# One transpose buffer instead of two, and all attention masks loaded at once as bf16

## What is computed

```python
def _L0_attn_ref(x, Wq, Wk, Wv, Wo, bo, Wconv):
    kc = conv_general_dilated(x.transpose(0,2,1), Wconv, window_strides=(3,), padding='VALID', ...)
    k_tmp = concatenate([x[:, :1, :], kc], axis=1)            # 1366 keys
    mask = (k_idx[None, :] * 3.0 >= q_idx[:, None] + 0.001)
    q, k, v = x @ Wq.T, k_tmp @ Wk.T, k_tmp @ Wv.T            # 16 heads of 64
    scores = einsum('bhqd,bhkd->bhqk', q, k) * HD ** (-0.5) + mask * -1000000000.0
    o = einsum('bhqk,bhkd->bhqd', softmax(scores), v)
    return o.reshape(b, t, d) @ Wo.T + bo
def _L0_ffn_ref(x, ...):                                      # w1, w2: 4096x1024; h1, h2: 4096x4096; w3: 1024x4096
    h = silu(tlin(x, w1_w, w1_s)) * tlin(x, w2_w, w2_s)
    h = gelu(tlin(h, h1_w, h1_s)); h = gelu(tlin(h, h2_w, h2_s))
    return tlin(h, w3_w, w3_s)
x = x + layernorm(_L0_attn_ref(layernorm(x), ...))
x = x + layernorm(_L0_ffn_ref(layernorm(x), ...))
```

## Time and profile before

| | us |
|---|---|
| median of the 2 runs | 6467.4 (6462.9 to 6471.9) |
| profiled execution | 6481.0 |
| its slowest core, core 3 (first to last instruction) | 6479.5 |
| its other cores | 6429.4 to 6447.9 |
| TensorE busy / VectorE / ScalarE, core 3 | 3206.5 / 705.8 / 599.9 |
| busy time of the 16 DMA engines, SP's queue / POOL's queue | 40.7% / 17.4% of the span |

### The profile page before, as it was taken

The page is one execution under the profiler, slowest core; times in us unless marked ns, Lnnn a source line. Parts: engine busy times, 40 slices in busy tenths (PEclk is TensorE's granted clock), DMA queues, the critical chain, the costliest instruction groups (busy, mean ns, idle before and its releaser), DMA issues.

```text
span 6479.5 us, 38888 instructions; the slowest of 8 cores (6429.4 to 6479.5 us)
## 1 busy us (share of the span) xinstructions
PE 3206.5 (49%) x15168; PEld 1447.2 (22%) x15168; DVE 705.8 (11%) x1430; ACT 599.9 (9%) x881; POOL 89.7 (1%) x176
## 2 busy tenths in 40 slices
PE   0000044651001020234425999489985999669994
PEld 0000011220000010112202444134432444224441
DVE  0014400101001010111044000110001100020001
ACT  0000000010001010223211100011000100011000
POOL 0000000000000000010000000000000000000000
PEclk9999987875555555555567999789997999889997
DMA  9963345339999999960244555256543555345552
GB/s 128 121 130 99 98 78 84 52 52 208 110 146 186 141 166 196 211 151 4 62 107 117 149 142 145 75 140 156 141 121 96 143 146 153 96 117 145 143 143 78
DMA packets 1378643, 805.86 MB, mean 124 GB/s; under 512 B 607248, under 2 KB 1338528, under 8 KB 1364128
## 3 DMA queue, kind: packets, MB, share of 16 engines
q1 hardware_dynamic: 1360352, 610.44, 40.7%
q0 software_dynamic: 18112, 192.95, 17.4%
HBM read 618.73 MB, written 236.98 MB: 132 GB/s over the span
## 4 chain that ended last, share of the span: by engine, by line
PE 46%; DMA 24%; another core or an unknown queue 11%; SPq 8%; DVE 4%; issue 4%; ACT 2%; DVEq 0%; POOL 0%; ACTq 0%; POOLq 0%
PE ps_f L1140 28%; PE ps_f L1078 6%; DMA p2b<-n_h 5%; DMA wbuf<-t_w 4%; PE ps_f L1198 4%; DMA t_h<-p2b 4%; PE ps_cv L462 3%; SPq L697 3%; DMA cv_nat<-wconv 2%; ACT pt_sb L802 2%; DMA lx<-x_full 2%; DVE ln_st L311 2%; SPq L450 1%; DMA p2b<-n_w 1%
## 5 line engine op out<-in xcount | busy, mean ns | idle before, releaser
L1140 PE MATMUL ps_f<-cslab,wbuf 128*128 128x512 bf16 x4096 | 893.0, 381 | 42.0 <-DMA wbuf<-t_h 42.0
L1140 PE MATMUL ps_f<-hslab,wbuf 128*128 128x512 bf16 x4096 | 892.8, 381 | 42.1 <-DMA wbuf<-t_h 42.1
L462 PE MATMUL ps_cv<-xwin,wt_cv 128*128 128x512 bf16 (+1 forms) x576 | 182.4, 482 | 1022.9 <-DMA wt_cv<-n_cv 1022.9
L818 PE MATMUL ps_oA<-vtm,pt_sb 128*128 128x65 bf16 x408 | 54.8, 237 | 1193.4 <-ACT pt_sb L802 1193.4
L1078 PE MATMUL ps_f<-x2fm,wbuf 128*128 128x512 bf16 x2048 | 455.5, 385 | 337.6 <-DMA wbuf<-t_w 337.1
L1140 PEld LDWEIGHTS ps_f<-cslab,wbuf 128*128 128x128 bf16 x4096 | 402.5, 98 | 532.5 <-issue 54.9
L1140 PEld LDWEIGHTS ps_f<-hslab,wbuf 128*128 128x128 bf16 x4096 | 402.3, 98 | 532.5 <-issue 54.9
L1198 PE MATMUL ps_f<-hslab,wbuf 128*128 128x512 bf16 x1024 | 258.0, 419 | 216.1 <-DMA wbuf<-t_w 216.1
L1078 PEld LDWEIGHTS ps_f<-x2fm,wbuf 128*128 128x128 bf16 x2048 | 201.0, 99 | 592.1 <-issue 362.3
L818 PEld LDWEIGHTS ps_oA<-vtm,pt_sb 128*128 128x128 bf16 x408 | 42.2, 126 | 1234.9 <-issue 1234.9
L462 PEld LDWEIGHTS ps_cv<-xwin,wt_cv 128*128 128x128 bf16 x576 | 59.3, 104 | 1145.5 <-issue 1125.7
(11 more groups left out here) (80 smaller groups left out, 1539.1 us busy)
## 6 DMA issues: line engine op xcount, KB each, us to landing
wbuf<-t_h SPq DMA_DIRECT2D x256, 1024.0 KB, 9.3
n_h<-h POOLq DMA_DIRECT2D x32, 2048.0 KB, 145.2
t_h<-p2b POOLq DMA_DIRECT2D x64, 1024.0 KB, 7.8
wbuf<-t_w SPq DMA_DIRECT2D x128, 512.0 KB, 5.4
wbuf<-t_w SPq DMA_DIRECT2D x32, 1024.0 KB, 8.2
n_w<-w POOLq DMA_DIRECT2D x16, 1024.0 KB, 162.1
lx<-x_full SPq DMA_DIRECT2D x32, 512.0 KB, 3.8
t_w<-p2b POOLq DMA_DIRECT2D x16, 1024.0 KB, 7.6
```

The source lines that it names most:

```text
L462: ins = t.matmul(ps_cv[ot][:, 0:pn], wt_cv_t(kd)[:, ot * 128:(ot + 1) * 128], xwin_t(kd)[:, w:3 * (pn - 1) + w + 1:3], start=(w == 0 and k ...
L818: t.matmul(po[:, 0:65], pt_sb[:, slot * 1536 + si * 256: slot * 1536 + si * 256 + 128], vtm_t(kt)[:, h * HW:(h + 1) * HW], start=first, st ...
L1140: ins = t.matmul(pb[mt][:, 0:TC], wbuf_t(par, k)[:, mt * 128:(mt + 1) * 128], src_t(k), start=(k == 0), stop=(k == DHT - 1))
```

## The change

- Both entries of `p2b` become the same buffer; the second is gone. Each DMA transpose now waits for `dPW0` and `dPW1`, so for the write of the step before it.
- `_mload` on SP, per pair, is gone. `_mload_all` on POOL issues all 16 mask loads ahead of the loop, into a bf16 tensor that holds them all (a cast on the way); it waits for `qfm`. All masked score tiles wait for all 16 loads.
- The order of the casts and of the p2 steps in the code is the same, so `_mload_all`, with its wait for `qfm`, stands in POOL's queue between `_prep` and the first 7 casts of h1.

```diff
@@ -641,8 +641,7 @@
 
         p2es = contextlib.ExitStack()
         p2b0 = p2es.enter_context(nc.sbuf_tensor("p2b0", [128, DH], BF16, side="right"))
-        p2b1 = p2es.enter_context(nc.sbuf_tensor("p2b1", [128, DH], BF16, side="right"))
-        p2b = [p2b0, p2b1]
+        p2b = [p2b0, p2b0]
         cast_q = {"h1": [(n_h1, h1, r0, "dgH1") for r0 in range(0, DH, 256)],
                   "h2": [(n_h2, h2, r0, "dgH2") for r0 in range(0, DH, 256)],
                   "w3": [(n_w3, w3, r0, "dgH2") for r0 in range(0, D, 256)]}
@@ -693,7 +692,8 @@
                     if i < 2:
                         wait(sy, "cA", ev["qfm"])
                     wait(sy, gate_, ev[gate_])
-                    wait(sy, f"dPW{par}", ev.get(f"p2w{par}", 0))
+                    wait(sy, "dPW0", ev.get("p2w0", 0))
+                    wait(sy, "dPW1", ev.get("p2w1", 0))
                     ev[f"p2t{par}"] = inc(sy.dma_start(
                         p2b[par][:, 0:O_], nat_[0:O_, kd_ * 128:(kd_ + 1) * 128],
                         transpose=True), f"dPT{par}")
@@ -713,18 +713,34 @@
             return list(range(_klo(2 * jp) // 128, _ktiles(2 * jp + 1)))
 
         MKP = max(len(_mk_pair(jp)) for jp in range(NJ // 2))
+        NMK = sum(len(_mk_pair(jp)) for jp in range(NJ // 2))
         a2 = contextlib.ExitStack()
         with a2:
             pt_sb = a2.enter_context(nc.sbuf_tensor("pt_sb", [128, 2 * 6 * 256], BF16, side="right"))
-            mk_sb = a2.enter_context(nc.sbuf_tensor("mk_sb", [128, 2 * MKP * 256], F32, side="right"))
+            mk_sb = a2.enter_context(nc.sbuf_tensor("mk_sb", [128, NMK * 256], BF16, side="right"))
             ps_scA = a2.enter_context(nc.psum_tensor("ps_scA", [128, 3 * 512], F32))
             ps_scB = a2.enter_context(nc.psum_tensor("ps_scB", [128, 3 * 512], F32))
             ps_oA = a2.enter_context(nc.psum_tensor("ps_oA", [128, 512], F32))
             ps_oB = a2.enter_context(nc.psum_tensor("ps_oB", [128, 512], F32))
             ps_sc = [ps_scA, ps_scB]
             ps_o = [ps_oA, ps_oB]
-            mk_slot = lambda jp, i: mk_sb[:, ((jp % 2) * MKP + i) * 256:
-                                          ((jp % 2) * MKP + i + 1) * 256]
+            mk_base = {}
+            _mb = 0
+            for jp_ in range(NJ // 2):
+                mk_base[jp_] = _mb
+                _mb += len(_mk_pair(jp_))
+            mk_slot = lambda jp, i: mk_sb[:, (mk_base[jp] + i) * 256:
+                                          (mk_base[jp] + i + 1) * 256]
+
+            def _mload_all(g):
+                wait(g, "cA", ev["qfm"])
+                for jp_ in range(NJ // 2):
+                    for i_, kt_ in enumerate(_mk_pair(jp_)):
+                        inc(g.dma_start(mk_slot(jp_, i_),
+                                        maskT[kt_ * 128:(kt_ + 1) * 128,
+                                              2 * jp_ * 128:(2 * jp_ + 2) * 128]), "dMK0")
+            bb.gpsimd(_mload_all)
+            ev["mload_all"] = cnt["dMK0"]
 
             gnum = 0
             itc = 0
@@ -732,21 +748,6 @@
                 mk = _mk_pair(jp)
                 j0 = 2 * jp
 
-                def _mload(sy, jp=jp, mk=tuple(mk), j0=j0):
-                    if jp == 0:
-                        wait(sy, "cA", ev["qfm"])
-                        wait(sy, "cV", ev["kfm"])
-                        wait(sy, "cV", ev["vtm"])
-                    if jp == 1:
-                        wait(sy, "cV", ev["consts"])
-                    if jp >= 2:
-                        wait(sy, "cA", ev.get(f"mask_used{jp - 2}", 0))
-                    for i, kt in enumerate(mk):
-                        inc(sy.dma_start(mk_slot(jp, i),
-                                         maskT[kt * 128:(kt + 1) * 128,
-                                               j0 * 128:(j0 + 2) * 128]), f"dMK{jp % 2}")
-                    ev[f"mload{jp}"] = cnt[f"dMK{jp % 2}"]
-                bb.sync(_mload)
                 emit_casts(7)
                 emit_p2(16)
 
@@ -781,7 +782,7 @@
                         if has_mask:
                             def _mask(v, jp=jp, g=tuple(g), psc=psc, mk=tuple(mk), gnum=gnum):
                                 wait(v, "cT", ev[f"scmm_g{gnum}"])
-                                wait(v, f"dMK{jp % 2}", ev[f"mload{jp}"])
+                                wait(v, "dMK0", ev["mload_all"])
                                 for si, kt in enumerate(g):
                                     if kt in mk:
                                         mi = list(mk).index(kt)
```

## The result

| | before | after |
|---|---|---|
| median of all runs | 6481.9 (18 runs) | 6417.4 (19 runs) |
| ratio | | 0.9904, 95% interval 0.9872 to 0.9935 |
| profiled execution | 6481.0 | 6395.3 |
| slowest core in it | 6479.5 (core 3) | 6393.5 (core 5) |

(In some executions the cores of one die run at a lower granted clock and the time is up to 7% longer, with either kernel; the ratios leave these out, the medians of the table hold them.) The forecast was 6717 us, 4% slower, range 6590 to 6980. The time fell by 86 us in the profiled executions, outside the range and to the other side.

A forecast was written before the change was run, and what follows sets the result against it. The chain of 112 p2 steps, then attention's tail, was taken to set the pace; -251 - 122 + 140 + 482 = +249, called +250, on 6481.0 gave 6731, or 6717 us against the runs' median; range 6590 to 6980.

The forecast's parts named there:

- wait for `otm`: SP's wait before the output projection: claimed to vanish once attention's masks leave SP's queue, -251 us.
- start without the seven casts: Convolution weight round trips at the start: without seven h1 casts beside them, everything after comes earlier, -122 us.
- the seven casts in the chain: Start of the p2 chain: the moved casts delay step 0's write, which step 1 now awaits, +140 us.
- w1, w2 gaps: Gaps between writes of p2 steps for w1 and w2: 15 lengthen from 9.77 to 15.0 us, +78 us.
- h gaps: Gaps between h1 and h2 writes outside cast bursts: 61 lengthen from 9.91 to 15.0 us, +310 us.
- w3 gaps: Gaps between the quarter-size w3 writes: 32 lengthen from 3.97 to 6.9 us, +94 us.
- attention's cover: Attention stage: done some 610 us into a stage the chain keeps open about 2090, so its extra work stays hidden.
- the last rival: p2 chain: keeps its pace because SP's buffer waits were short, only attention's room counts; 6234 us, chance 2%.
- one buffer: p2 chain: transpose, write and next transpose follow each other, lengthening the steps of w1, w2, h and w3; +482 us.
- the first rival: p2 chain: a transpose alone is much faster than its engine share says, step 11.2 us; 6398 us, chance 10%.
- upper rival: p2 chain: landings don't shorten when transfers run alone, step 18.9 us; 7096 us, chance 10%.
- my 15.0: Big p2 step with one buffer, in us: transpose 9.6, write 4.8, handover 0.6; between bounds 13.7 and 18.9.

## Why the prediction was wrong, step by step

| term | predicted | measured |
|---|---|---|
| wait for `otm` | -251 | -251 (SP doesn't wait) |
| start without the seven casts | -122 | -136 (first transpose 1444.2 to 1308.0) |
| the seven casts in the chain | +140 | +137 (147.2 less a gap of 9.8) |
| w1, w2 gaps | +78 | +31 (14 x 2.2) |
| h gaps | +310 | +74 (61 x 1.21) |
| w3 gaps | +94 | +74 (32 x 2.30) |
| gaps with casts | 0 | -8 |
| sum | +249 | -79, and the chain of the profile shows 3088 - 3165 = -77 |

**What held.** The reading of the stage (chain of transposes first, attention's tail behind it), both moves of the casts, attention's cover, and that SP would not wait for `otm`. The run with the casts back in the start shows that their two effects cancel. Of the 328 us of error, 283 are in w1, w2 and h, and 20 in w3. Attention's own work was put at 593 us and is 732: the 1114.7 us of mask waits include 133.0 of idle time ahead of the first addition. Under a cover of over 1000 us this changed nothing. "Chain first, then the tail" is true of the sum, but attention, from the masks ahead of w3 on, was what ran last, as the run with one buffer and nothing else shows. And the last rival counted as waits for a buffer only those for `t_h`; there were 123.0 us in 39 more for `t_w`.

**What failed** is one term, "one buffer", put at +482 us and measured at +179: the length of a serial step, and in it one number, the transpose alone: "6.44 + 2.4 = 8.8", called a lower bound, and 9.6 taken. It landed in 6.1. Two things were wrong.
- The 6.44 us came from a DMA share with a write in flight beside the transpose, and I took it for the work of the transpose. Alone the share gives 4.98 us, and the second of two in a row adds 4.4 to 5.6. One buffer takes the company away, so the number that I carried over was measured in the state which the change ends.
- The 2.4 us of latency came from small transposes in a row, issued 1.2 us apart. A big one ended 1.1 us above its engine time.

The row that told it was there: SP issued an h transpose in as little as 3.9 us. I had used it for the first rival, computed 11.2 us a step and 6398 us from it, and gave it 10%. What I set against it, the first transpose with its 11.1 us, was no transpose alone: a second was issued behind it 7 us later, two mask loads went ahead, and its own issue took 6.9 us. The run with one buffer and nothing else has it without the second one: 7.04 us. And one core was too few to read. On core 4 of the kernel before, the same transpose, with the same company, was there to be read at 6.93 us:

```profile
1432.85 6.93 DMA p2b<-n_w
```

The steps of w1 and w2 in the changed kernel are also slower than the later ones of h, 11.95 against 11.0 (11.35 when it was measured again), as are the first of h, 11.4. With the writes on SP, where the first of these steps comes only after 2030 us, near attention's end, w1 and w2 take 10.6 and h 10.4. So the slower ones go with attention running beside them, not with the weight; by which resource, no run here tells.

The rules of the Trainium skill ("DMA: Bandwidth & Descriptors": 261 GB/s for a DMA transpose in "Latency and other measured facts", 2.0 us plus bytes at 436 GB/s in "Anatomy of one DMA") had given, as the prediction's estimate from that page, 6.0 and 4.4 us for the two transfers and 11.0 for the step. The page fits the 2.0 us to DMAs issued by GpSimd; to add them to a transpose from SP was the prediction's own step. The trace of the kernel after has 6.1, 4.2 and 11.0. The prediction let the row decide against it, and the row was of another state.

**Why two buffers gain so little.** With two buffers the two transfers share the engines: they land in 9.5 and 7.4 us instead of 6.1 and 4.2, and a pair takes 9.9 in the kernel before and 10.0 in the changed one with two buffers. In turn it takes 11.1. Overlap wins about 1 us of a big step, not a transfer, and 2.3 of a step of w3; I take this to be the latencies and the handover, which is argued from the sizes and not shown apart. So the change gave up 145 us (by the ratios) to 179 us (by the table) here, and won 251 by unhooking attention. The upper rival (18.9) and my 15.0 both rest on the same mistake: that a transfer measured in company keeps its length without it.

## What to carry to other kernels

Here a DMA's landing time and its engine share, read while another transfer was in flight, were upper bounds of what it took alone; look for the fastest instance, on all cores, and for its issue time, before calling a share a floor. With the engines busy for 90% with two streams, the second buffer hid little of the big transfers, and to serialise them cost as little; what paid was to move bulk transfers to a stage where the engines are free: 16 casts cost 19 us in all there, and 300 beside the transposes. A cast's 19 us are themselves a figure read in company: it was 13 where the cores were out of step. And loads that gate compute shouldn't stand in one queue with a long chain of transfers that nothing near needs.

## What the runs showed that I had not expected

A bulk cast starves a transpose in another queue: with 36 casts (2 MB written each) outstanding, one transpose of 1 MB stood for 653 us in its issue. Two transposes in a row don't disturb each other (6.15 us to landing for the second), while a transpose and a write side by side take as long as one after the other (10.6 and 8.7 against 6.1 + 4.2). And cores without any traffic between them seem to slow each other's casts: 166 GB/s against 108 to 118, at the same full engine share.
